# Expert weights released per chunk, a two-pass last up tile, and an earlier row sum

## The reference

```python
x = x + ffn0(cond0(x, cond_128, ...))     # grouped 9-tap convolution, then ffn0
x = x + ffn1(cond1(x, cond_128, ...))     # a mixed 64 x 64 kernel per sample, then ffn1

def ffn0(x1):                             # H = 2752 hidden units, D = 1024
    w_up   = dequant_nf4(codes_up, absmax_up)      # (H, D), absmax per 64 values
    w_down = dequant_nf4(codes_dn, absmax_dn)      # (D, H)
    x2 = relu(x1 @ w_up.T + b_up + x1 @ up_lora_a @ up_lora_b)
    return x2 @ w_down.T + b_down + x2 @ dn_lora_a @ dn_lora_b

def ffn1(x):                              # 8 experts, each row goes to one
    selected = argmax(softmax(x @ gate_w.T + gate_b))
    return expert_w[selected] @ x + expert_b[selected]
```

## Time and profile before

| what | value |
|---|---|
| median of 3 runs | 1411.74 us (1407.86 to 1414.0) |
| profiled execution, its own time | 1414.34 us |
| its span, first to last instruction | 1412.4 us |
| TensorE busy | 1384.3 us (98%) |
| VectorE busy | 1136.7 us (80%) |
| ScalarE busy | 755.1 us (53%) |
| mean granted TensorE clock | 0.998 |

### The profile page before, as it was taken

One profiled execution on the slowest core, in us unless ns is written; L12 is line 12 of the kernel. 1 busy time (PEld: TensorE's weight loads), 2 busy tenths in 40 slices (PEclk: granted clock), 3 DMA queues, 4 the chain that ended last, 5 costly groups with the idle time before them and its releaser, 6 DMA issues.

```text
span 1412.4 us, 20755 instructions
## 1 busy us (share of the span) xinstructions
PE 1384.3 (98%) x6881; PEld 1140.5 (81%) x6881; DVE 1136.7 (80%) x1119; ACT 755.1 (53%) x839; POOL 210.4 (15%) x234
## 2 busy tenths in 40 slices
PE   7999999999999999999999999999999999999988
PEld 7988888888888888888888888888766788788877
DVE  6968887878878788887887878877655699899887
ACT  6655554545545454455545455553204277687764
POOL 0110000000000000000000000000014266456444
PEclk9999999999999999999999999999999999999999
DMA  6953756568664776747667477764858756959962
GB/s 213 361 226 143 264 207 245 195 255 261 235 259 180 274 251 225 277 162 291 228 241 272 166 287 228 254 259 165 295 190 300 275 140 170 348 176 304 340 185 43
DMA packets 103083, 331.51 MB, mean 235 GB/s; under 512 B 15493, under 2 KB 23181, under 8 KB 103021
## 3 DMA queue, kind: packets, MB, share of 16 engines
q1 hardware_dynamic: 79700, 258.56, 49.2%
q0 software_dynamic: 23072, 71.85, 18.2%
q10 hardware_dynamic: 256, 0.40, 0.1%
HBM read 295.63 MB, written 46.14 MB: 242 GB/s over the span
## 4 chain that ended last, share of the span: by engine, by line
PE 88%; DMA 4%; DVE 3%; issue 2%; ACT 1%; SPq 1%; DVEq 0%; POOL 0%; ACTq 0%; POOLq 0%
PE pair L1151 26%; PE pair L1152 25%; PE pair L1153 25%; PE pair L1207 4%; DMA wraw<-exp_w 3%; PE pair L1355 1%; DVE wlr L1126 1%; PE pair L1346 1%; PE pair L1429 1%; DVE wf L815 1%; PE pair L1396 1%; PE pair L1234 1%; PE pair L1291 1%; PE pair L1217 1%; PE pair L1364 1%
## 5 line engine op out<-in xcount | busy, mean ns | idle before, releaser
L815 DVE TENSOR_TENSOR wf<-wf,term 128x1024 f32<-128x1024 f32 x308 | 376.7, 1223 | 66.5 <-ACT term L601 51.5
L601 ACT ACTIVATE term<-codes 128x1024 f32<-128x1024 int32 x308 | 320.7, 1055 | 141.1 <-DVE wf L815 141.1
L1151 PE MATMUL pair<-wh,hh 128*128 128x512 f32 x672 | 263.4, 392 | 3.2 <-DVE ring L878 1.4
L1152 PE MATMUL pair<-wl,hh 128*128 128x512 f32 x672 | 262.0, 390 | 0.0
L1153 PE MATMUL pair<-wh,hl 128*128 128x512 f32 x672 | 261.9, 390 | 0.0
L1151 PE MATMUL pair<-ring,wh 128*128 128x512 f32 x656 | 255.5, 390 | 0.0
L1152 PE MATMUL pair<-ring,wh 128*128 128x512 f32 x656 | 255.3, 389 | 0.0
L1153 PE MATMUL pair<-ring,wl 128*128 128x512 f32 x656 | 255.2, 389 | 0.0
L748 ACT ACTIVATE whr<-wraw 128x1024 fp32r x184 | 188.0, 1056 | 90.1 <-PE pair L1153 39.2
L873 DVE TENSOR_TENSOR acc<-acc,pair 128x1024 f32<-128x1024 f32 x160 | 194.4, 1216 | 47.0 <-PE pair L1153 39.7
L1126 DVE TENSOR_TENSOR wlr<-wraw,whr 128x1024 fp32r<-128x1024 f32 x184 | 213.8, 1216 | 15.4 <-ACT whr L748 15.2
(11 more groups left out here) (180 smaller groups left out, 1505.5 us busy)
## 6 DMA issues: line engine op xcount, KB each, us to landing
ring<-x_parts SPq DMA_DIRECT2D x320, 512.0 KB, 6.2
wraw<-exp_w SPq DMA_DIRECT2D x64, 512.0 KB, 15.4
x_parts<-stage POOLq DMA_DIRECT2D x24, 512.0 KB, 6.8
xg<-exp_b POOLq DMA_DIRECT2D x23, 512.0 KB, 8.2
codes<-codes_up SPq DMA_DIRECT2D x22, 512.0 KB, 5.9
codes<-codes_dn SPq DMA_DIRECT2D x22, 512.0 KB, 5.7
am<-am_dn SPq DMA_DIRECT2D x22, 512.0 KB, 3.9
acc<-x_nat POOLq DMA_DIRECT2D x16, 512.0 KB, 5.4
```

Source lines behind the costliest of these rows:

```text
L601: return nc.scalar.activation(out, codes[:, n % 2], ACT.Relu, scale=scale, bias=-scale * bend)
L815: nc.vector.tensor_tensor(whole(n), whole(n), term[:, e % 2], op).then_inc(term_added, 1)
L1151: mm(ps, ah, bh, start=first, stop=False)
L1152: mm(ps, ah, bl, start=False, stop=False)
```

## The change

**Weights by chunk.** The wait for the old expert moves into `load_expert`: chunk kt waits until that chunk of the old expert's last tile has been converted, not for all eight. `wlr_ready` starts at 8 instead of 1, so that `through` still fits, and `product`'s wait is rewritten to match.

**Two passes.** Once, after the second tile of the last unit is split, VectorE copies its low part's columns 64 to 127 over the same columns of the high part (`pack_halves`): 64 columns of high, 64 of low. `up` with `last` then needs two matmuls per stretch for that tile, with the activations' high and low parts. Bank 1 holds high products in one half of the rows and low products in the other. ScalarE copies each half to the other's rows of a scratch tile `turned` (`turn_halves`), and VectorE adds it (`sum_halves`), so both halves hold the full sum. Then `relu` goes on. The low by low product, which was left out before, is now in the sum.

**Row sum.** In the last unit, VectorE takes a job's first row sum between the sum of halves and `hidden_low` of the next job. To place these steps, round 4 is taken out of the loops of TensorE, VectorE and ScalarE and written out.

```diff
@@ SyncE @@
-            def load_expert(e):
+            def load_expert(e, done=0):
                 for kt in range(KT):
                     if e > 1:
-
+                        sp.wait_ge(wlr_ready, done + kt)
                         sp.wait_ge(wraw_in[e % 2][kt], 16 * (e // 2 + e % 2))
...
-                done = sp.value_load(through[0:1, e - 1:e], min_val=1, max_val=NS * KT + 1)
-                sp.wait_ge(wlr_ready, done)
-                load_expert(e)
+                load_expert(e, sp.value_load(through[0:1, e - 1:e], min_val=1, max_val=NS * KT + 1))
@@ ScalarE @@
+            def turn_halves(q):
+
+                act.wait_ge(up_mm, JOBS - NC + q + 1)
+                wait(act, summed, q)
+                for c in range(2):
+                    rows, other = slice(c * 64, c * 64 + 64), slice(64 - c * 64, 128 - c * 64)
+                    nc.scalar.activation(turned[rows], bank[1][other], ACT.Copy).then_inc(turned_ready, 1)
...
+                if last:
+                    turn_halves(q % NC)
                 for s in range(2):
+                    if s and last:
+                        act.wait_ge(summed, q % NC + 1)
@@ VectorE @@
+            def pack_halves():
+
+                dve.wait_ge(wl_ready, JOBS - 2)
+                high, low_ = (part(1).rearrange("p (k n) -> p k n", n=P)[:, :, 64:P] for part in (high_part, low_part))
+                nc.vector.tensor_copy(high, low_).then_inc(packed_ready, 1)
+
+            def sum_halves(q):
+                dve.wait_ge(turned_ready, 2 * (q + 1))
+                nc.vector.tensor_tensor(bank[1], bank[1], turned[:], ALU.add).then_inc(summed, 1)
...
-            for i in rounds(dve, UNITS // 2):
+            for i in rounds(dve, UNITS // 2, last=True):
...
-                        if k % 4 != 2:
+                        if final and k == 7:
+                            add_ramps(i, k + 4, range(2, 6))
+                            sum_halves(0)
+                            add_ramps(i, k + 4, (6,))
+                            add_down(i, k, 0)
+                        elif k % 4 != 2:
...
+                    sum_halves(k + 1)
+                    add_down(UNITS // 2, k, 0)
                     hidden_low(UNITS // 2, k + 1)
...
-                for j in range(CT):
+                for j in range(int(k < NC - 1), CT):
                     add_down(UNITS // 2, k, j)
...
-            dve.sem_inc(wlr_ready, 1)
+            dve.sem_inc(wlr_ready, KT)
@@ TensorE @@
+                        if s and last:
+                            mm(bank[s], high_part(n)[:, c], parts[:, kt, 0], start=kt == 0, stop=False)
+                            ins = mm(bank[s], high_part(n)[:, c], parts[:, kt, 1], start=False, stop=kt == KT - 1)
+                            continue
...
-                    pe.wait_ge(wlr_ready, i * 32 + KT * s + kt + 2)
+                    pe.wait_ge(wlr_ready, i * 32 + KT * (s + 1) + kt + 1)
```

More of the change, by code:

```diff
@@ L188, in program @@
         bup = sb(late, "bup", [P, NT])
+        turn = ExitStack()
+        turned = sb(turn, "turned", [P, CHUNK])
+        turn.close()
         xcv0 = sb(late, "xcv0", [P, 2, GROUPS, MB])
@@ L273, in program @@
         up_mm, relu_done, hh_ready, hl_ready = sem("up_mm"), sem("relu_done"), sem("hh_ready"), sem("hl_ready")
+        packed_ready, turned_ready, summed = sem("packed_ready"), sem("turned_ready"), sem("summed")
         dn_mm, acc_added = sem("dn_mm"), sem("acc_added")
@@ L630, in high, with relu @@
                 nc.scalar.activation(high_part(n), whole(n), ACT.Copy).then_inc(wh_ready, 1)
-            def relu(i, q):
+            def turn_halves(q):
[4 more added lines that the diff above has]
+                    nc.scalar.activation(turned[rows], bank[1][other], ACT.Copy).then_inc(turned_ready, 1)
+            def relu(i, q, last=False):
                 act.wait_ge(up_mm, i * 8 + q + 1)
                 act.sem_inc(act_passed, 1)
+                if last:
+                    turn_halves(q % NC)
                 for s in range(2):
+                    if s and last:
+                        act.wait_ge(summed, q % NC + 1)
                     nc.scalar.activation(bank[s], bank[s], ACT.Relu,
@@ L691, in _ @@
                 conv_high(k)
-            for i in rounds(act, UNITS // 2):
+            for i in rounds(act, UNITS // 2, last=True):
                 for k in range(8):
-                    early = isinstance(i, int) and k == 0
+                    early = isinstance(i, int) and i == k == 0
                     if not early and k % 4 in (0, 3):
@@ L706, in _ @@
                     if not early:
-                        relu(i, k + 1)
+                        relu(i, k + 1, isinstance(i, int) and i > 0 and k == 7)
                     ramps(i, k + 4, (7,))
@@ L713, in _ @@
             high(UNITS // 2, 3)
-            relu(UNITS // 2, 1)
+            relu(UNITS // 2, 1, True)
             perceptron(0)
             perceptron(1)
-            relu(UNITS // 2, 2)
+            relu(UNITS // 2, 2, True)
             perceptron(2)
-            relu(UNITS // 2, 3)
+            relu(UNITS // 2, 3, True)
             for g in range(2):
@@ L866, in add_down @@
                     return
-                if j == 0 and q >= NC and not isinstance(i, int):
+                if j == 0 and q >= NC and not (isinstance(i, int) and i == 0):
                     dve.wait_ge(acc_in[q - NC], i * 16)
@@ L935, in _ @@
                 conv_low(k)
-            for i in rounds(dve, UNITS // 2):
+            for i in rounds(dve, UNITS // 2, last=True):
                 for k in range(8):
-                    if isinstance(i, int) and k == 0:
+                    final = isinstance(i, int) and i > 0
+                    if isinstance(i, int) and i == k == 0:
                         add_ramps(i, k + 4, (1,))
@@ L960, in _ @@
                             low(i, k + 3)
+                            if final and k == 6:
+                                pack_halves()
                             add_ramps(i, k + 4, (6,))
                         hidden_low(i, k + 1)
-                        add_down(i, k, 0)
+                        if not (final and k == 7):
+                            add_down(i, k, 0)
                         add_ramps(i, k + 4, (7,))
@@ L1235, in lora_product, with up @@
                 ins.then_inc(ab_mm, 1)
-            def up(i, q, between=None, halves=None):
+            def up(i, q, between=None, halves=None, last=False):
                 pe.wait_ge(wl_ready, i * 8 + 4 * (q // 4) + 2)
+                if last:
+                    pe.wait_ge(packed_ready, 1)
                 wait(pe, hl_ready, i * 8 + q)
@@ L1319, in _ @@
                 conv(k)
-            for i in rounds(pe, UNITS // 2):
+            for i in rounds(pe, UNITS // 2, last=True):
                 for k in range(8):
-                    if isinstance(i, int) and k == 0:
+                    if isinstance(i, int) and i == k == 0:
                         up(i, k + 1, (0, 3)).then_inc(up_mm, 1)
@@ L1328, in _ @@
                     else:
-                        up(i, k + 1, halves=(i, k + 3) if k % 4 == 2 else None).then_inc(up_mm, 1)
+                        up(i, k + 1, halves=(i, k + 3) if k % 4 == 2 else None,
+                           last=isinstance(i, int) and i > 0 and k == 7).then_inc(up_mm, 1)
                     down(i, k, (i, k + 4))
@@ L1332, in _ @@
                 if k < NC - 1:
-                    up(UNITS // 2, k + 1).then_inc(up_mm, 1)
+                    up(UNITS // 2, k + 1, last=True).then_inc(up_mm, 1)
                     perceptron(2 * k)
```

## The result

The changed kernel takes 1400.05 us (median; 1396.98 to 1401.73), the kernel before 1412.68 us in the runs beside it: a ratio of 0.9913, 95% interval 0.9892 to 0.9933. Forecast were 1401.6 us and a gain of 12.7; the profiled execution went from 1414.34 to 1401.73 us, 12.6 us. That sum is right, but both of its terms were mis-sized, in opposite directions. The first transformed rows (the product of `acc` and the mixed kernels that follows the last unit) start at 1053.11 us instead of 1059.28, 6.2 us where 4.6 were forecast. The expert stage, from its first tile's first matmul to its last one's end, takes 274.9 us instead of 280.7, 5.7 where 8.1 were forecast. The rest, 0.7 us, lies between the two and goes with TensorE's clock.

A forecast was written before the change was run, and what follows sets the result against it. TensorE was taken to bound the kernel (88% of the last-ending chain), with some waits for late weights. 1414.34 - 8.1 (expert stage) - 4.6 (last unit) = 1401.6 us, range 1396.5 to 1409.

The forecast's parts named there:

- (2): Expert stage: weights bound by DMA throughput, not load start; 3 us won instead of 8.1, 1406.7 us; chance 0.16.
- (4): Expert stage: release does nothing, SyncE reaching each wait late; last unit gains little too; 1413.4 us; chance 0.03.
- The bound of 9.1 us: Expert stage: most that earlier weights can win, 7.4 us of TensorE idle time and 1.7 us of lowered clock.
- The term of 8.1 us: Expert stage: gain from chunkwise release, 9.1 less 0.4 for a remaining gap and 0.6 for another bias-row wait.
- a sign that the prediction had set for itself: Expert stage: the forecast is wrong if tiles stay further apart than 11.9 us on average.
- one more of them, perhaps a little longer, I price at 0.6 us: Expert stage: earlier loads meet GpSimd's transfers; one more VectorE wait for a bias row costs 0.6 us.
- The lead that was to take most of such a wait: Expert stage: VectorE runs some 3.0 us ahead of TensorE and takes most of a bias-row wait.
- rival (3): Expert stage: early weights crowd the DMA engines, bias rows exceed their 15.4 us; slower, 1435.6 us; chance 0.05.
- Job 40's loss: Last unit: the down product's fourth block waits some 0.7 us for the second row sum, leaving 1.1 of 1.8.
- Here 2.0 us of the 2.9 saved so far turn into a wait for the bias rows.: Last unit, job 40's down product: third block cannot start before 997.8 us, costing 2.0 us of the saving.
- the 4.6 us: Last unit: net gain of the two passes, 7.2 us of matmuls less waits; bounds 0.9 and 8.5 us.
- rival (1): Last unit gives almost nothing, 0.9 us: bias wait and VectorE's order hold it; 1405.3 us; chance 0.13.

The follow-up runs named there:

- bias row between: Changed kernel, but GpSimd issues the next tile's bias row between a tile's two gathers instead of behind both: 1397.59 us, ratio 0.9908.
- release alone: Kernel before, with only the weights' release per chunk added and the old last unit kept: 1405.99 us, ratio 0.9958.
- bias row first: Changed kernel, but GpSimd issues the next tile's bias row ahead of both gathers instead of behind them: 1418.22 us, ratio 1.0036.
- down bias first: Changed kernel, but SyncE loads the down bias as the first of ten constants instead of the last: 1397.24 us, ratio 0.9892.
- row sum behind the split: Changed kernel, but VectorE's first row sum in the last unit stands behind the split again, as before: 1406.63 us, ratio 0.9965.
- passes and row sum alone: Changed kernel with the old release of the weights, all eight chunks at once: 1404.73 us, ratio 0.9950.

## Why the prediction was right, and where it was not

**What bounds the kernel, and the release.** The view held: the losses of the stage were TensorE's waits, nearly all for late weights, and the clock behind them. Loads issued from 1187.94 over 9.4 us, no clock below 1.00 in the stage, two large gaps gone: rivals (2) and (4) fall. The bound of 9.1 us was 1.1 too low, because the idle time in brackets isn't all that a wait costs. In the changed kernel tiles start at 1215.60, 1228.09 (0.54 idle) and 1240.00, 24.40 us for two tiles, 0.28 more than 2 x 11.79 + 0.54. Four such waits make up 1.1 of the 10.2 us between the 280.7 before and the 270.5 of bias row between.

The term of 8.1 us is near the mean of four kernels with the release (7.6 us by the stages of their profiles); the medians give 6.5 for the release alone, and the changed kernel's own profile 5.7. There the stage's part fails by a sign that the prediction had set for itself, tiles further apart than 11.9 us on average: they stand 12.0 us apart (12.26 before).

**The step that was mis-sized in the stage** is "one more of them, perhaps a little longer, I price at 0.6 us". There were five more, and TensorE's idle time was 2.9 us instead of 1.0; that is 1.9 of the 2.4 us missing. The other 0.5 is the cost beside the brackets: one wait more than before (0.3), a tile 0.1 late with no idle time in its bracket (1275.36 to 1287.26), and 1.6 instead of 1.7 us for the clock.

The lead that was to take most of such a wait was too large as well. The step had VectorE 3.0 us ahead, from one wait (3.35 less 0.38); in the changed kernel the bias waits of 1.76, 1.12, 2.52, 2.61 and 1.96 us left 0.19, 0.37, 0.54, 1.44 and 0.36 us of idle time, so the lead was 0.8 to 2.0.

The budget behind it was wrong too. The 15.4 us of rival (3) came from a bias row issued 8.2 us after the row sum two tiles before it, the bias of a tile that did not wait. The wait itself belongs to a row behind two held issues, in the kernel before already: issued 1301.36 - 1286.76 = 14.6 us after its row sum.

```profile
1286.76 1.21 DVE L1120 TENSOR_TENSOR xg<-xg,pair 128x1024 f32<-128x1024 f32 x1
1301.36 1.00 POOL L543 DMA_DIRECT2D xg<-exp_b  x1
```

In the changed kernel the row that is late at 1269.43 was issued 1259.54 - 1244.89 = 14.65 us after that row sum; two tiles are 2 x 11.35 = 22.7 us, so it had 8.05 us, took 9.9 to land, and was 1.8 late. Rival (3)'s mechanism was there, with a nearer threshold than it was given, and in part on another resource: GpSimd's issue, not the DMA engines alone. VectorE's lead, six waits instead of eleven and their length (1.1 to 2.6 us) kept it small, so its 1435.6 us did not come. The one slower order, bias row first (1418.2), is slow by another wait, TensorE's for gathered rows, which no rival had.

**The two passes** saved 7.3 us of matmuls for 7.2. Job 40's loss (0.8 for 0.7) and job 43's (0.5 for 0.4) are as worked out. The down product that covers the copies was put at 8.2 us; it takes 9.36 without a wait (down bias first), so the cover is wider than the prediction has it.

**The step that was mis-sized in the last unit** is "Here 2.0 us of the 2.9 saved so far turn into a wait for the bias rows." The mechanism is right (down bias first removes the wait), the size was 0.65. The step took the landing of before, 991.08, plus 0.25, and said it couldn't come earlier. It came at 989.84. SyncE's issues of the constants before, and then after:

```profile
980.99 1.90 SPq L404 DMA_DIRECT2D b0s<-b  x1
```

```profile
981.09 0.43 SPq L408 DMA_DIRECT2D b0s<-b  x1
...
984.05 0.44 SPq L409 DMA_DIRECT2D bdn<-bias_dn  x1
```

One issue of the nine had taken 1.9 us in the trace that I read, where the others take 0.3 to 0.4; the down bias behind it was 1.4 us late by that the earlier trace rows. It is not the accident of one execution: the release alone, which keeps the old last unit, has it too, and the nine kernels with two passes, where this issue takes 0.43 to 0.44 us, don't.

```profile
980.96 1.48 SPq L404 DMA_DIRECT2D b0s<-b  x1
```

What held it isn't known. In the seven other profiles that load the down bias last it landed between 988.5 and 990.3 us. The 1.3 us too much here, and 0.3 at job 41's product, make the 4.6 us into 6.2; rival (1) falls.

**The sum.** +1.6 and -2.4 us, and the 0.7 us of clock between the two parts that was not forecast, nearly cancel. The forecast was made against the profiled execution and meets that of the changed kernel to 0.1 us and the median to 1.5; with such terms that is in part luck. Both terms lie within the bounds that were set for them (0 to 9.1 and 0.9 to 8.5 us).

## What to carry to other kernels

When a wait is removed, ask for each transfer that becomes the next to be late how long after its trigger it was issued in the tiles where it was late, not in a quiet one, and whether the trace shows it held. Before an issue is moved ahead in an in-order queue, look at what it waits for there and who wants what is then behind it: the same bias row cost 18 us ahead of both gathers, and between them the stage of the profile was 4.5 us shorter. A slow row in the trace (1.9 us among nine issues of 0.4) is to be named as a doubt where a term rests on it, since the change may take it away. And a wait costs more than the idle time in its bracket, here 0.3 us more.

## What the hardware showed beyond that

- Some of GpSimd's DMA issues take as long as the run of VectorE subtracts with two SBUF operands beside them: 3.45 us beside three, 5.83 beside five, mostly 1.0 to 1.2 otherwise; it is in the kernel before too (five issues over 5 us). Of those that begin in such a run, 27 of 43 are not held in the changed kernel. What decides it is open.
- After idle times of 1.8 and 2.3 us TensorE's granted clock fell to half for 3.4 us (row sum behind the split), and not after 1.58 us in the same kernel. In the kernel before it fell after 2.91 us and not after 2.61; in passes and row sum alone it fell after 2.41 us (0.83 over 1217 to 1227 us) and not after 2.77 (1.00 over 1366 to 1376). So the length of one wait doesn't decide it alone; what does is not settled by these runs.
